# Counting both relations of a graph layer in one number, parted by bytes

## The reference

```python
norm_x = weight * (x * rsqrt(mean(x * x) + 1e-6))
out = norm_x @ W_root + bias
for r in range(2):
    w = (edge_type == r).astype(x.dtype)
    msg = norm_x[src] @ W_rel[r] * w[:, None]
    sums = segment_sum(msg, dst, num_segments=N)
    cnt = segment_sum(w, dst, num_segments=N)
    out = out + sums / maximum(cnt, 1.0)[:, None]
...
agg = segment_sum(h[src], dst, num_segments=n)      # in each of the three later layers
```

## Time and profile before

| | us |
|---|---|
| median of 3 runs | 584.37 |
| lowest and highest | 583.69, 584.87 |
| profiled execution, its own time | 585.49 |
| its span | 583.7 |

### The profile page before, as it was taken

One profiled execution on the slowest core, in us unless ns is written; L12 is line 12 of the kernel. 1 busy time (PEld: TensorE's weight loads), 2 busy tenths in 40 slices (PEclk: granted clock), 3 DMA queues, 4 the chain that ended last, 5 costly groups with the idle time before them and its releaser, 6 DMA issues.

```text
span 583.7 us, 8611 instructions
## 1 busy us (share of the span) xinstructions
PE 566.7 (97%) x2704; PEld 410.8 (70%) x2704; DVE 380.4 (65%) x980; ACT 231.7 (40%) x477; POOL 100.6 (17%) x80
## 2 busy tenths in 40 slices
PE   6999999999999999999999999999999999999992
PEld 3566666566578898987898888877868867455541
DVE  7599988888837898988512330028748667755455
ACT  5444455533224546463321221013223233366555
POOL 3000000000000000003164512302202230132230
PEclk8999999999999999999999999999999999999997
DMA  8500111111031121129300000600100100021123
GB/s 261 154 26 13 35 35 35 35 35 35 0 89 40 37 62 46 46 71 247 128 20 0 0 0 1 226 1 1 38 1 0 36 0 1 1 71 52 54 70 105
DMA packets 20961, 30.74 MB, mean 53 GB/s; under 512 B 5458, under 2 KB 15404, under 8 KB 20928
## 3 DMA queue, kind: packets, MB, share of 16 engines
q1 hardware_dynamic: 20512, 29.66, 17.1%
q10 hardware_dynamic: 416, 0.67, 0.4%
HBM read 25.20 MB, written 5.12 MB: 52 GB/s over the span
## 4 chain that ended last, share of the span: by engine, by line
PE 92%; DMA 3%; DVE 3%; ACT 1%; SPq 0%; issue 0%; DVEq 0%
PE banks L745 20%; PE banks L949 12%; PE banks L1035 12%; PE banks L868 10%; PE banks L731 5%; PE banks L836 5%; PE banks L971 4%; PE banks L961 4%; PE banks L897 4%; PE banks L899 4%; PE banks L878 3%; PE banks L1025 3%; PE banks L739 1%; PE banks L853 1%; DMA w_all<-in_L_gnn_W_rel 1%; DMA cb_b<-in_L_gnn_conv_bias 1%
## 5 line engine op out<-in xcount | busy, mean ns | idle before, releaser
L745 PE MATMUL banks<-w_all,xnT 128*125 128x429 f32 x320 | 130.4, 532 | 2.3 <-DMA w_all<-in_L_gnn_W_rel 2.3
L745 PEld LDWEIGHTS banks<-w_all,xnT 128*125 128x125 f32 x320 | 54.6, 190 | 32.5 <-issue 29.7
L1198 DVE TENSOR_TENSOR adj<-adj,banks 125x220 f32 x160 | 60.9, 381 | 19.5 <-PE banks L731 17.4
L868 PE MATMUL banks<-hT,w_s 128*128 128x250 f32 x320 | 69.0, 375 | 0.2
L868 PEld LDWEIGHTS banks<-hT,w_s 128*128 128x128 f32 x320 | 60.2, 189 | 8.8 <-issue 1.4
L897 PE MATMUL banks<-y_hi,adj 125*125 125x288 f32 x200 | 55.2, 304 | 0.4 <-issue 0.4
L731 PEld LDWEIGHTS banks<-oh_code,oh_low 125*128 125x128 bf16 x320 | 31.0, 97 | 32.0 <-issue 27.9
L899 PE MATMUL banks<-y_lo,adj 125*125 125x286 f32 x200 | 53.5, 294 | 0.0
L1180 DVE TENSOR_TENSOR oh_code<-iota_c,edge 125x880 bf16<-125x880 f16 x80 | 48.9, 611 | 0.0
L1342 DVE TENSOR_SCALAR hT<-banks,g_c,b_c 128x125 f32<-128x125 f32 x60 | 19.4, 401 | 45.0 <-PE banks L853 45.0
L949 PE MATMUL banks<-adj,h_hi 125*128 125x250 f32 (+1 forms) x180 | 48.3, 367 | 0.1
(11 more groups left out here) (206 smaller groups left out, 896.8 us busy)
## 6 DMA issues: line engine op xcount, KB each, us to landing
xt<-in_x SPq DMA_DIRECT2D x15, 448.0 KB
out_x<-ot SPq DMA_DIRECT2D x9, 448.0 KB
w_s<-in_L_gnn_W SPq DMA_DIRECT2D x5, 512.0 KB, 6.4
xn<-in_x SPq DMA_DIRECT2D x5, 448.0 KB
wd_s<-in_L_gnn_Wd SPq DMA_DIRECT2D x1, 2048.0 KB, 12.1
w_all<-in_L_gnn_W_rel SPq DMA_DIRECT2D x6, 286.0 KB, 6.8
wo_s<-in_L_gnn_wo_weight SPq DMA_DIRECT2D x1, 1024.0 KB, 6.2
w_all<-in_L_gnn_W_root SPq DMA_DIRECT2D x3, 286.0 KB, 6.4
```

Of the source, the lines that this page charges most:

```text
L745: ins = pe.matmul(pb[0:P, 2 + 2 * v + n, 0:FH], xnT[:, u], w_all[:, u, n * FH:(n + 1) * FH], start=(u == 0), stop=(u == KD - 1))
L868: ins = pe.matmul(pb[:, b0 if f == 0 else 4 + f % 2, 0:2 * P], w1_s[:, k, f * 128:(f + 1) * 128], hT[:, k], start=(k == 0), stop=(k == KD ...
L1198: dve.tensor_tensor(cols, cols, window(b, q), ALU.add).then_inc(done, 1)
```

## The change

Both relations are counted in one fp32 number. A new name `cnt` is the memory of `adj`'s relation 0. It is set to 2^23 in place of zero, and an edge adds 1 to it if it is of relation 0 and 256 if it is of relation 1. In such a number the lowest byte is the count of relation 0 and the second byte that of relation 1. `e_mark` goes; `e_val` (1 or 256) is computed in its place, turned by TensorE (four transposes more) and copied by ScalarE to `value`. The one-hot of codes has 110 columns in place of 220 (compare, 440 elements), and is then multiplied in place by the edge's value (440 elements), which waits for the compare (`codes_set`). A count has 110 columns, an addition 110 elements. ScalarE clears three times in the loop and no longer ahead of it, and five times (`part`) reads the bytes of 250 finished columns and writes them as numbers: byte 1 to relation 1, then byte 0 in place to relation 0, each 2500 elements. The first of them comes in tile 4, then in 6, 8 and 9, the last behind the last `evacuate`. TensorE waits for `parted` ahead of every second destination tile of `relations`. The tests are extended: no two half rows may overlap by more than a node, every quarter row must span more than one node, and the parted columns must be finished. The slow path keeps its own names (`far_count`, `far_window`).

```diff
+SECOND = 256.0
+UNITS = float(2 ** 23)
+DONE = 2 * P
...
+        cnt = at(top[0], "cnt", [P, T, ND], F32)
+        digits = cnt[:].bitcast(U8).rearrange("p t (n b) -> p t n b", b=4)
...
         def window(b, q):
+            return pb[0:P, b, q * C:(q + 1) * C].rearrange("p (b w) -> p b w", w=W)
...
+            def part(k, cols):
+                act.activation(adj[:, 1, :, cols], digits[:, :, cols, 1:2].rearrange("p t n o -> p t (n o)"),
+                               ACT.Copy).then_inc(second_set, 1)
+                act.wait_ge(second_set, k + 1)
+                act.activation(adj[:, 0, :, cols], digits[:, :, cols, 0:1].rearrange("p t n o -> p t (n o)"),
+                               ACT.Copy).then_inc(parted, 1)
...
                 if cleared is not None:
-                    filled(1 - v, bass.ds(cleared, CS), CS).then_inc(adj_rest, 1)
+                    filled(bass.ds(cleared, CS), CS).then_inc(adj_rest, 1)
+                if complete is not None:
+                    act.wait_ge(counts_free, complete * (2 * UG) + 2 * UG + 2)
+                    part(complete, bass.ds(complete * DONE, DONE))
                 evacuate(t, v)
...
-            filled(0, slice(0, C0), C0).then_inc(adj_zero, 1)
+            act.wait_ge(edges_ps, 1)
+            act.copy(value[:, 0:G], pb[0:P, 4, 160:160 + J * G].rearrange("p (j g) -> p g j", j=J)).then_inc(far_copied, 1)
...
-            tile_of_1(T - 1, 1, None, True)
+            tile_of_1(T - 1, 1, None, True, None, T // 2 - 2)
+            act.wait_ge(counts_free, G + 2)
+            part(T // 2 - 1, slice(N - DONE, N))
...
+                        ins = pe.matmul(pb[:, b, q * C:(q + 1) * C], oh_low[:, b, q, :, j],
+                                        oh_both[:, b, q, :, j], start=(j == 0), stop=(j == JH - 1))
...
                     pe.wait_ge(edges_ready, 1)
+                    pe.wait_ge(prep, 9)
+                    turn_edges(4, e_val, 160)
                     turn_edges(1, e_code).then_inc(edges_ps, 1)
...
+                    if t % 2 == 0:
+                        pe.wait_ge(parted, t // 2 + 1)
...
-            dve.tensor_copy(adj[:, 1, :, 0:C0], zeros(C0)).then_inc(adj_zero, 1)
+            dve.memset(cnt[:, :, 0:C0], UNITS).then_inc(adj_zero, 1)
...
-            step(dve.scalar_tensor_tensor(e_mark[:], typ_i[:], 0.5, e_blk[:], ALU.mult, ALU.add))
+            dve.tensor_scalar(e_val[:], typ_i[:], SECOND - 1.0, 1.0, ALU.mult, ALU.add)
...
-            def codes(g, b, code):
+            def codes(g, b):
-                return dve.tensor_tensor(oh_code[:, b], both(iota_c, R * C), spread_out(code, g, R * C), ALU.is_equal)
+                return dve.tensor_tensor(oh_both[:, b], both(iota_m, C), spread_out(edge[:, 1], g, C), ALU.is_equal)
+            def weighed_codes(g, b):
+                dve.wait_ge(codes_set, g + 1)
+                return dve.tensor_tensor(oh_both[:, b], oh_both[:, b], spread_out(value, g, C), ALU.mult)
...
-                    cols = adj[:, :, :, bass.ds(base[q], W)]
+                    cols = cnt[:, :, bass.ds(base[q], W)]
...
                     if more:
+                        codes(g + 2, b).then_inc(codes_set, 1)
                         lows(g + 2, b)
                     dve.wait_ge(first_added, g + 1)
                     place(base, b, 1, placed, counts_free)
                     if more:
-                        codes(g + 2, b, edge[:, 1]).then_inc(onehots, 1)
+                        weighed_codes(g + 2, b).then_inc(onehots, 1)
```

120 lines of the change are left out of this document (74 added, 46 removed).

## The result

The kernel became faster: 576.12 us median of 4 runs (575.35 to 578.05) against 584.09 us (583.69 to 584.87) for the kernel before on the same chip. The ratio is 0.9862, 95% interval 0.9844 to 0.9880, a gain of 8.0 us. Four more runs of it on another occasion gave 576.50 us and the ratio 0.9876 (0.9851 to 0.9900). The profiled execution took 575.35 us by its own time, 573.5 of them in its span; before it was 585.49 us, so the profiled pair shows 10.1 us, more than the medians. Forecast were 573.7 us and a range from 572.3 to 580.5.

A forecast was written before the change was run, and what follows sets the result against it. TensorE was taken to bound the counting loop, VectorE having some 12% of slack. Gains of 11.7 less 0.4 (transposes) and 0.6 (VectorE's holds) made 10.7 us, median 573.7 us; the 8-in-10 range was 572.3 to 580.5.

The forecast's parts named there:

- The counts: TensorE's counting loop: 110 columns take a count to about 52 ns, 138 or 178 ns saved a row, 11.7 us in all.
- The 105 ns behind the last count: TensorE's loop: the projection behind the last count can't start effectively earlier than some 105 ns after it, as now.
- What is added on TensorE: First tile: four more transposes of 80 columns add 0.40 us; VectorE's extra preparation, an estimated 1.2 us, doesn't show.
- The new row: VectorE's counting loop: a row takes between 1.46 and 1.71 us, taken as 1.55, a wait standing ahead of the register load.
- rival A: Counting loop: VectorE paces, at a row of 1.66 us a tile needs 15.44, time 579.5 us; chance 0.20.
- The engine's own sum: VectorE's row without its queue: two additions, two compares and the multiplication take 1.38 us of engine time.
- The 0.34 of GpSimd's turn: VectorE's tile: time in which GpSimd's subtraction holds a compare up, averaged from 78 compares of 512 in the earlier trace.
- ScalarE: Five pairs of byte conversions, 4.7 us each, replace three fills and stay covered, the last by half a microsecond.
- Rival D: ScalarE's last conversions: reading bytes with a stride of four takes twice the time, about 4.2 us bare, 578 us; chance 0.06.
- B: TensorE's counts are paced by weight loads or issue, not columns: 577.1 us at 68 ns, 584.8 at 98; chance 0.08.
- C: VectorE's 440-element operations run at half rate, row 1.84 us, time 594 us; decides from 1.72; chance 0.04 including the slow path.
- E: The new tests send the kernel down the slow path, costing milliseconds; chance under 1%.

## Why the prediction was right, and where it was not

**The counts: right.** Forecast were 52 ns a count, a row of 1.71, TensorE's tile of 14.70 and 11.7 us in all. Measured: 52 ns, 1.71, 14.70, and 141.60 - 129.95 = 11.65 us in the kernels that let TensorE pace. The argument from the earlier trace rows, that a load record of 97 ns doesn't mean 97 ns of the array, held down to 28 ns. The rule of the Trainium skill weighed there (TensorE: Matmul & The Clock Gate, "Back-to-back issue gap", about 81 ns a matmul at 128 columns) isn't what this kernel shows: 52 ns at 110 columns, 28 at 55, in groups of four counts between fp32 matmuls. One detail was off: "0.27 us and not 0.40" for four counts and the way to the projection was 0.21. The 105 ns behind the last count do exist, since the row lost 0.14 us and not 0.18, but they show in the projections (four take 1.66 us by the merged record, where they took 1.61) and not ahead of them.

**What is added on TensorE: right.** Forecast 0.4 us, measured 0.43, and nothing of VectorE's preparation shows, as forecast.

**VectorE: right in the row, wrong in the sum, and this is the step that failed.** The new row was forecast at 1.55 us and measured at 1.56. The next step said "A tile needs of VectorE ... 14.45 us; of TensorE ... 14.70. TensorE stays the bound, by 0.25 us". It needs 15.04. Three terms of it were off: 0.09 for nine rows that are 0.01 longer; 0.22 for GpSimd's turn, 0.56 and not 0.34 (why, below); and 0.28, half of the loop's turn, which wasn't in the sum at all. The kernel before makes the same turn, but there VectorE waited for TensorE anyway, so no row of its trace called for a price. So rival A is what happened, at less than half the size that it was given: VectorE paces from the second tile on, and the lag costs 2.8 us and not 0.6. The reason given for its row, a wait ahead of the register load, was only half of it. The run that put the load ahead of the wait changed nothing; those that took the wait's steps out of the queue made the row 1.35 to 1.40. It is the length of the queue that counts. The engine's own sum was off as well, 1.38 and not 1.29: it took the multiplication's whole record where the other terms leave out the overlap of 0.08. That did no harm in the forecast, as the queue set the row, but it spoiled the expectation of the run with one more multiplication.

The 0.34 of GpSimd's turn came from a trace in which VectorE had slack. There the turn found VectorE waiting for TensorE in five of nine tiles, so that only its last part could hold anything up, and in three more a compare already under way, which went on unhindered. The timeline of the kernel before, of GpSimd and VectorE:

```profile
107.05 1.20 POOL L375 TENSOR_TENSOR y_lo<-y_f,y_hi 125x572 fp32r<-125x572 f32 x1 [15.01 <-ACT y_f L458]
107.46 0.38 DVE L1198 TENSOR_TENSOR adj<-adj,banks 125x220 f32 x1 [0.73 <-PE banks L731]
107.76 0.77 DVE L1176 TENSOR_TENSOR oh_low<-iota_l,edge 125x512 bf16<-125x512 f16 x1
```

The compare of the sources was the only operation held up, by 0.09 to 0.98 us. In the kernel after VectorE no longer waits: in each of the nine tiles one of the two compares or the multiplication begins under the turn and is lengthened by 0.55 to 1.00 us, of which the row, in a settled tile, shows 0.56.

**ScalarE: right.** Conversions of 2.3 us, a pair in 4.7, cover at the end 0.5 forecast and 0.75 measured, and the stretch behind the last count unchanged at 417.8 us. Rival D is out.

**The other rivals.** B is out by the spacings at three widths. C asked for a half-rate multiplication; it took 0.38, as the compare of its shape. Its threshold was misplaced, though: with 1.00 us in a tile beside the rows, the loss begins at a row of (14.70 - 1.00) / 9 = 1.52 us, and the gain is gone at (16.03 - 1.00) / 9 = 1.67, not 1.72. At 1.59, with the extra multiplication, the loop kept 5.3 us of its 11.65. E didn't occur.

**The sum.** Forecast was 10.7 us off, and the pair of profiled executions shows 10.1. That nearness is luck. The loop gave 8.9 and not 11.1, and the start gave 1.3 where -0.4 was forecast, because the profiled execution of before had a clock dip in its start. Without the start's scatter the change costs 0.43 us there and gives 8.9 in the loop, 8.45 in all. That fits what the runs show: the medians differ by 8.0 and 7.4, the lowest times (575.35 after, 583.38 to 583.69 before) by 8.0 to 8.3. The median of after missed the forecast of 573.7 by 2.4 us, and 2.2 of them are the lag behind VectorE that was priced at 0.6 and came to 2.8. Of the runs of after 5 of 8 lie 1 us or more above the lowest, of those of before 11 of 31; from so few it can't be told whether the change makes late starts more frequent.

## What to carry to other kernels

A margin of 0.25 us in a tile of 14.7 is no margin: before calling an engine the second, add up its whole cycle, the loop's turn and other engines' disturbance included, over the period in which these recur, and not its average. An engine whose records show the same small gap ahead of one instruction in each row is paced by its own queue: count the queue's steps (register loads, waits against registers, each its own instruction in a loop), and write the loop out where that engine is the limit; here that one line gave 3 us more and the fastest kernel that computes the reference, 573.2 us. And compare the starts of two traces before reading their difference as the change's.

## What the runs showed of the hardware

- A 128-column bf16 weight load is recorded with 97 ns, yet count matmuls follow each other by 98, 52 and 28 ns with 220, 110 and 55 columns.
- A wait against a register's value is an instruction of its own in VectorE's queue, with another that computes the value; both are 40 ns by their records, and in the run without them the row went from 1.56 to 1.40 us. Against a constant it is part of the waiting instruction.
- One and the same program got the full clock at 7.2 us in one execution and at 11.7 in another, worth 0.96 us at the first count. Over all kernels with this start it was 6.1 to 15.0 us, and the first count moved by up to 2.6. Ahead of that time the view's granted clock said 1.00, where matmuls 0.72 us apart, and 0.36 later, showed the low level.
- GpSimd's subtraction of 572 fp32 elements (1.2 us) lengthens a two-byte operation of VectorE that begins beside it from 0.38 to as much as 1.20 us; with the subtractions moved behind the loop no such operation of the loop is lengthened.
- A register load of VectorE took 0.53 us for two registers, and for four 0.34 to 0.36 us in some tiles and 0.96 to 0.97 in others.
- Idle time of TensorE costs more than itself: 3.9 us of wait became 6.0, with 6.8 us at granted clock 0.5 behind it; a wait of 14 us brought 13.65 us at that level.
- ScalarE reads bytes with a stride of four at its usual rate: 2500 elements in 2.3 us, where the fills take 2.72 for 3000.
